# Statistics over two neighbouring tiles an instruction, the last two tiles loaded by channel halves, and a reordered start of the first layer

## The reference, cut to what matters

```python
def _gn(v, G=32, eps=1e-5):                       # mean and variance of an image over H, W and 12 channels
    g = v.reshape(B_, H_, W_, G, C_ // G)
    m = jnp.mean(g, axis=(1, 2, 4), keepdims=True)
    s = jnp.var(g, axis=(1, 2, 4), keepdims=True)
    return ((g - m) / jnp.sqrt(s + eps)).reshape(v.shape)

def conv_ref(x):                                  # WINDOW = (1, 5, 20), zero padded
    s = box_sum(x, 2, 5)                          # along the width
    num = box_sum(s * s, 3, 20)                   # along the channels
    d = box_sum(box_sum(x * x, 2, 5), 3, 20)
    denum = d * norm[None, :, :, None]            # norm: how many pixels of the width a window covers
    return jnp.nan_to_num(num / denum, nan=1.0)

x = x + conv_ref(_gn(x))                          # layer 0
x = x + conv_ref(_gn(x))                          # layer 1
```

## Time and profile before

| | before |
|---|---|
| median of 3 runs | 6088.15 us (6087.32 to 6090.02) |
| span of the profiled execution | 6085.2 us |
| TensorE busy | 5723.6 us (94%) |
| ScalarE busy | 5014.0 us (82%) |
| VectorE busy | 4144.7 us (68%) |
| GpSimd busy | 3546.7 us (58%) |
| DMA | 1007.81 MB, mean 166 GB/s |
| start of the first width unit | 323.31 us |
| start of the first channel unit | 331.46 us |

### The profile page before, as it was taken

The page is one execution under the profiler, slowest core; times in us unless marked ns, Lnnn a source line. Parts: engine busy times, 40 slices in busy tenths (PEclk is TensorE's granted clock), DMA queues, the critical chain, the costliest instruction groups (busy, mean ns, idle before and its releaser), DMA issues.

```text
span 6085.2 us, 139173 instructions
## 1 busy us (share of the span) xinstructions
PE 5723.6 (94%) x49196; PEld 5710.7 (94%) x49196; DVE 4144.7 (68%) x9033; ACT 5014.0 (82%) x8201; POOL 3546.7 (58%) x1043
## 2 busy tenths in 40 slices
PE   0089999999999999999999999999999999999999
PEld 0089999999999999999999999999999999999999
DVE  9988889988877766767667555555555555555555
ACT  0078888888888888888888888888888888888888
POOL 0056665566556666666665666666666666666665
PEclk9999999999999999999999999999999999999999
DMA  9946655556633433434334344343434434343343
GB/s 367 367 157 212 223 207 191 207 203 215 220 125 125 151 138 134 156 124 153 137 135 147 132 147 143 129 160 124 159 130 141 149 124 165 124 153 137 135 154 124
DMA packets 660641, 1007.81 MB, mean 166 GB/s; under 512 B 5168, under 2 KB 660528, under 8 KB 660528
## 3 DMA queue, kind: packets, MB, share of 16 engines
q1 hardware_dynamic: 660528, 1006.65, 47.1%
HBM read 603.98 MB, written 402.65 MB: 165 GB/s over the span
## 4 chain that ended last, share of the span: by engine, by line
PE 89%; DVE 8%; issue 2%; ACT 1%; DMA 0%; SPq 0%; DVEq 0%; POOL 0%; POOLq 0%; ACTq 0%
PE width_ps L468 43%; PE den_ps L492 23%; PE num_ps L492 23%; DVE out_stats L555 3%; DVE lane_mv L562 2%; DVE y_out L649 1%; DVE newton L631 1%; DVE recip L637 0%; DMA y_out<-in_x_dram 0%; DVE beside_stats L555 0%; ACT recip L398 0%; ACT recip L401 0%; SPq L198 0%; DVEq L555 0%; PE num_ps L443 0%
## 5 line engine op out<-in xcount | busy, mean ns | idle before, releaser
L312 POOL TENSOR_TENSOR centred<-x_in,mean_row 128x1536 f32<-128x1536 f32 x512 | 1771.0, 3459 | 1415.0 <-PE width_ps L468 1097.5
L321 POOL TENSOR_TENSOR y_out<-x_in,y_out 128x1536 f32<-128x1536 f32 x512 | 1771.4, 3460 | 1117.1 <-DVE y_out L649 1117.1
L631 DVE SCALAR_TENSOR_TENSOR newton<-den_ps,recip 128x384 f32<-128x384 f32 x2048 | 1110.7, 553 | 1884.7 <-ACT recip L401 1854.8
L492 PE MATMUL den_ps<-band_c,tT 128*128 128x138 f32 (+2 forms) x12288 | 1809.0, 283 | 9.6 <-DVE newton L631 9.6
L492 PE MATMUL num_ps<-band_c,sT 128*128 128x138 f32 (+2 forms) x12288 | 1732.6, 284 | 20.4 <-DVE recip L637 20.1
L468 PE MATMUL width_ps<-band_w,centred 128*128 128x130 f32 x12288 | 1628.3, 275 | 0.5 <-DVE rvar_col L620 0.5
L468 PE MATMUL width_ps<-band_wc,square 128*128 128x130 f32 x12288 | 1625.5, 275 | 0.0
L492 PEld LDWEIGHTS den_ps<-band_c,tT 128*128 128x128 f32 x12288 | 1608.9, 190 | 13.3 <-DVE newton L631 11.8
L492 PEld LDWEIGHTS num_ps<-band_c,sT 128*128 128x128 f32 x12288 | 1580.5, 190 | 27.7 <-DVE recip L637 22.9
L388 ACT ACTIVATE sT<-width_ps,rstd_col 128x512 f32<-128x512 f32 x1536 | 1035.8, 674 | 592.9 <-PE width_ps L468 592.9
L468 PEld LDWEIGHTS width_ps<-band_w,centred 128*128 128x128 f32 x12288 | 1507.0, 191 | 0.9 <-DVE rvar_col L620 0.9
(11 more groups left out here) (44 smaller groups left out, 302.8 us busy)
## 6 DMA issues: line engine op xcount, KB each, us to landing
x_in<-in_x_dram SPq DMA_DIRECT2D x80, 3072.0 KB, 11.0
first_layer_out<-y_out SPq DMA_DIRECT2D x64, 3072.0 KB, 18.2
x_in<-first_layer_out SPq DMA_DIRECT2D x64, 3072.0 KB, 10.9
out_dram<-y_out SPq DMA_DIRECT2D x63, 3072.0 KB, 18.1
beside<-in_x_dram SPq DMA_DIRECT2D x30, 3072.0 KB, 11.0
y_out<-in_x_dram SPq DMA_DIRECT2D x18, 3072.0 KB, 24.4
out_dram<-y_out SPq DMA_DIRECT2D x4, 768.0 KB, 3.5
```

What stands on the lines that cost most here:

```text
L312: nc.gpsimd.tensor_tensor(centred[e % 2][:], x_in[slot][:, g * PSEG:(g + 1) * PSEG, :], mean_row[ph % 2][:].unsqueeze(1).to_broadcast([P, ...
L321: nc.gpsimd.tensor_tensor(y_out[slot][:, g * PSEG:(g + 1) * PSEG, :], x_in[slot][:, g * PSEG:(g + 1) * PSEG, :], y_out[slot][:, g * PSEG:( ...
L492: last = nc.tensor.matmul(bank[:, lo:hi], data[:, k, at:at + P], band_c[k][:], start=(k == 0), stop=(k == KB - 1), skip_group_check=True)
L631: nc.vector.scalar_tensor_tensor(newton[:, i, :], den_ps[i % 3][:, 0:C], TINY, recip[par][:, i, :], ALU.add, ALU.mult).then_inc(den_used, 1)
```

## The change

It has these parts.

1. `x_in` and `y_out` become halves of `x_both` and `y_both` (same bytes, same places). In the opening one `bn_stats` reads both tiles of a buffer pair, 32 segments by 12 channels = 384 elements, in place of 192. VectorE waits for both tiles, and `tile_measured` now counts tile pairs; both buffers of a pair are given back together, when the pair is measured.
2. `opening_totals` takes the place of `lane_totals` in the opening: `bn_aggr` reads 48 numbers a group in place of 96.
3. The last two tiles (tile pair 15) are loaded by two transfers that each bring half of the channels (16 groups) of both tiles, in pieces of 768 bytes where the others move 1536 at a time. VectorE measures and folds the first 16 groups, then the other 16.
4. The loads of image 1's first tiles (`y_out[0]`, `beside`, `y_out[1]`) wait for `means_asked` 1, that is for the end of the opening's totals; before, each `y_out` waited for its buffer to be measured.
5. GpSimd centres row pair 1 only after `params_ready`. ScalarE does the squares of row pair 1 after the takes of row pair 0's first two channel blocks.
6. TensorE runs the first width unit of row pair 0 ahead of round 3 of the hand-over and the others right behind it; its wait for `params_ready` comes after all six. ScalarE's takes still wait for `params_ready`.

```diff
--- before.py
+++ after.py
@@ -59,6 +59,7 @@
     assert W == 2 * P and C == 3 * P and TILES % 4 == 0 and B == 2 and TILES >= 8
 
     SPLIT = TILES // 2
+    CUT = GROUPS // 2
     MID = SPLIT // 2
 
 
@@ -86,9 +87,12 @@
         def sem(name):
             return ctx.enter_context(nc.semaphore(name))
 
-        x_in = [sb(f"x_in{i}", [P, SEGS, C]) for i in range(2)]
-        y_out = [sb(f"y_out{i}", [P, SEGS, C]) for i in range(2)]
+        x_both = sb("x_both", [P, 2 * SEGS, C])
+        y_both = sb("y_both", [P, 2 * SEGS, C])
+        x_in = [x_both[:, i * SEGS:(i + 1) * SEGS, :] for i in range(2)]
+        y_out = [y_both[:, i * SEGS:(i + 1) * SEGS, :] for i in range(2)]
         stat_tiles = [x_in[0], x_in[1], y_out[0], y_out[1]]
+        stat_pairs = [x_both, y_both]
         centred = [sb(f"centred{i}", [P, PSEG, C]) for i in range(2)]
         square = [sb(f"square{i}", [P, PSEG, C]) for i in range(2)]
         sT = [sb(f"sT{i}", [P, KB, 2 * W]) for i in range(2)]
@@ -192,16 +196,23 @@
 
                 def measure_loads(i, lo):
                     for s in range(4):
-                        if lo > 0:
-
-                            sp.wait_ge(tile_measured, i * 4 + s - 3)
+                        if lo > 0 and s % 2 == 0:
+
+                            sp.wait_ge(tile_measured, i * 2 + s // 2 - 1)
+                        if lo == TILES // 4 - 1 and s >= 2:
+                            continue
                         sp.dma_start(stat_tiles[s][:], view[:, bass.ds((i * 4 + s) * SEGS, SEGS), :]
                                      ).then_inc(in_landed[s], 16)
-                looped(sp, TILES // 4, measure_loads, [0])
+                looped(sp, TILES // 4, measure_loads, [0, TILES // 4 - 1])
+
+                for part in range(2):
+                    cs = slice(part * CUT * CG, (part + 1) * CUT * CG)
+                    sp.dma_start(y_both[:, :, cs], view[:, (TILES - 2) * SEGS:TILES * SEGS, cs]
+                                 ).then_inc(in_landed[2 + part], 16)
 
                 for s in range(2):
 
-                    sp.wait_ge(tile_measured, TILES - 3 + s)
+                    sp.wait_ge(tile_measured, TILES // 2 - 1)
                     sp.dma_start(x_in[s][:], tiles_of(x, 0)[:, s * SEGS:(s + 1) * SEGS, :]
                                  ).then_inc(in_landed[s], 16)
                 def load_beside(n):
@@ -212,7 +223,7 @@
 
                 for s in range(UPFRONT):
 
-                    sp.wait_ge(tile_measured, TILES - 1 + s)
+                    sp.wait_ge(means_asked, 1)
                     sp.dma_start(y_out[s][:], tiles_of(x, 1)[:, s * SEGS:(s + 1) * SEGS, :]
                                  ).then_inc(in_landed[2 + s], 16)
                     if s == 0:
@@ -324,6 +335,8 @@
                                             ALU.subtract).then_inc(rows_out, 1)
 
                 centre(0, 0, 0, 0)
+
+                pool.wait_ge(params_ready, 1)
                 centre(0, 1, 0, 1)
                 for ph in range(NP_):
                     def tiles(i, lo):
@@ -415,12 +428,13 @@
                             take(ph1, p1, 1 - par, n, int(what[0] == "T"))
 
                 finish_logs(0)
-                for p in range(2):
-                    for half in range(2):
-                        squares(0, p, p, half)
+                for half in range(2):
+                    squares(0, 0, 0, half)
                 for k in range(KB):
                     take(0, 0, 0, k, 0)
                     take(0, 0, 0, k, 1)
+                    if k < 2:
+                        squares(0, 1, 1, k)
                 for ph in range(NP_):
                     def pairs(i, lo):
                         step(ph, i * 2, 0)
@@ -512,13 +526,15 @@
                         elif ph1 < NP_:
                             width_unit(ph1, p1, 1 - par, n, int(what[0] == "T"))
 
-                for part in (1, 2, 3):
+                for part in (1, 2):
                     finish_part(0, part)
-
-                pe.wait_ge(params_ready, 1)
                 for k in range(KB):
                     width_unit(0, 0, 0, k, 0)
+                    if k == 0:
+                        finish_part(0, 3)
                     width_unit(0, 0, 0, k, 1)
+
+                pe.wait_ge(params_ready, 1)
                 for ph in range(NP_):
                     def pairs(i, lo):
                         step(ph, i * 2, 0)
@@ -562,14 +578,35 @@
                         last = nc.vector.bn_aggr(lane_mv[b][:, half, g, :], stats[:, g, :])
                     link(last)
 
+                def opening_totals(half, groups):
+
+                    for g in groups:
+                        last = nc.vector.bn_aggr(lane_mv[0][:, half, g, :], out_stats[:, g, 0:SPLIT // 2 * 6])
+                    link(last)
+
+
+                def measure_two(base, i, s):
+
+                    for o in range(2):
+                        dve.wait_ge(in_landed[2 * s + o], (base + i + 1) * 16)
+                    measure(stat_pairs[s], range(GROUPS), out_stats, i * 2 + s).then_inc(tile_measured, 1)
 
                 for half in range(2):
-                    with dve.Fori(0, SPLIT // 4) as i:
-                        for s in range(4):
-                            dve.wait_ge(in_landed[s], (half * (SPLIT // 4) + i + 1) * 16)
-                            measure(stat_tiles[s], range(GROUPS), out_stats, i * 4 + s).then_inc(tile_measured, 1)
-                    dve.wait_ge(tile_measured, (half + 1) * SPLIT)
-                    lane_totals(0, half, range(GROUPS), out_stats)
+                    with dve.Fori(0, SPLIT // 4 - half) as i:
+                        for s in range(2):
+                            measure_two(half * (SPLIT // 4), i, s)
+                    if half == 0:
+                        dve.wait_ge(tile_measured, SPLIT // 2)
+                        opening_totals(0, range(GROUPS))
+
+                measure_two(SPLIT // 4, SPLIT // 4 - 1, 0)
+                for part in range(2):
+                    groups = range(part * CUT, (part + 1) * CUT)
+                    dve.wait_ge(in_landed[2 + part], TILES // 4 * 16)
+                    link(measure(y_both, groups, out_stats, SPLIT // 2 - 1))
+                    if part == 0:
+                        dve.wait_ge(tile_measured, TILES // 2 - 1)
+                    opening_totals(1, groups)
 
 
                 dve.wait_ge(bands_cut, 2 * HALVES + KB + 1)
@@ -721,7 +758,7 @@
 
                 dve.wait_ge(in_landed[2], (TILES // 4 + 1) * 16)
                 measure(y_out[0], range(GROUPS), beside_stats, 0).then_inc(tile_measured, 1)
-                dve.wait_ge(tile_measured, TILES + 1)
+                dve.wait_ge(tile_measured, TILES // 2)
                 for ph in range(NP_):
                     def tiles(i, lo):
                         for e in range(BODY):
```

## The result

The changed kernel takes 6078.42 us (median of 21 runs, 6077.46 to 6080.48) against 6087.15 us (21 runs, 6086.51 to 6090.15): ratio 0.9985, 95% interval 0.9978 to 0.9991. The gain is 8.7 us; 3.9 were forecast. The forecast time was 6084.2 us, 5.8 above what was measured: 4.8 of these are gain that was not forecast, and 1.0 is the kernel before, whose median of 3 runs (6088.15) stood 1.0 above that of the 21 runs here. The profiled execution has a span of 6078.8 us.

The account below looks back on a forecast made before the run. The opening, in which TensorE idles, was taken as bound by a buffer pair's round trip. Opening 1.1 us sooner plus hand-over 2.8 gave -3.9 us, 6084.2 us; own range 6078 to 6091, 8 in 10 within 6072 to 6101.

Parts of the forecast that it names:

- One instant decides: Whole kernel: the change is worth the shift of the first channel unit, from 331.46 to 327.5 us, -3.9 us.
- D0: First channel unit, at 331.46 us in the kernel before, behind which every engine goes on as before; forecast at 327.5.
- Prices: Opening on VectorE: 461 ns for statistics over 384 elements, 14.8 us a tile pair; 255 ns for totals over 48 numbers.
- The rival of a price by the instruction: Opening's totals: 64 totals stay at 450 ns each, +12.5 us, 6096.7 us; chance 0.20.
- the one of statistics that don't shorten: Opening's statistics: a cost for each of 16 segments, not for the instruction; +16.7 us, 6100.9 us; chance 0.06.
- The round trip binds: Opening: a buffer pair is measured, reissued and landed in 34.8 us for two tile pairs, 17.4 us a tile pair.
- L: Opening's loads: time from issue to landing of a buffer pair's two tiles, taken as 19.9 us, between 19.4 and 20.4.
- The last part: Opening's last tile pair: both halves there when VectorE needs them; opening ends at 309.9 us, not 311.0, gain 1.1 us.
- Hand-over: From the opening's end to the first channel unit: 20.4 us becomes 17.6, a gain of 2.8 us.
- Part 4: Later loads of image 1: VectorE waits 1.5 us for `y_out[0]`; cost nothing, but later arrivals show one to one.
- a sign of being wrong: After the opening: `newton` waiting for `y_out[0]` would show the forecast wrong; the first `newton` was due at 329.9 us.
- The rival in which the DMA never runs dry: Opening's loads: issue overlaps the running pair, so 16 pairs pass at 16.87 us; -22 us, 6066 us; chance 0.11.

Follow-up runs that it names:

- experiments 1 and 2: Changed kernel with a third buffer pair: 6070.95 us; changed kernel with two 192-element statistics for each of 384, buffers still given back by pairs: 6096.16 us.
- experiment 5: Parts 5 and 6 undone in the changed kernel: 6081.88 us; added to the kernel before, both 6085.01, part 5 alone 6085.13, part 6 alone 6086.94.
- experiments 6 and 8: Changed kernel, second centring started at the reciprocal roots: 6077.35 us; kernel with three buffer pairs, spread first-half totals and earlier image 1 loads: 6070.38 us.

## Why the prediction was right, and where it was short

- *One instant decides.* Right: the shift of D0 (9.1) is the shift of the medians (8.7) to within their 1 us, and in every experiment too. The time lies at the lower edge of the forecast's own range (6078 to 6091), and the gain is more than twice the forecast: the mechanism was right and its sizes were not, and all three misses below err the same way.
- *Prices.* Statistics of 384 elements: forecast 461 ns and 14.8 us a pair; measured 14.81. Totals: 255 ns forecast, 232 measured; 64 of them are 1.5 us. The rival of a price by the instruction is out, and so is the one of statistics that don't shorten.
- *The round trip binds.* Right in kind, shown by experiments 1 and 2. L was forecast at 19.9; on the path it was 19.4 to 19.7, mostly 19.55, nearly the lower bound, one tile's trip plus one more transfer. A round was 34.5 for 34.8: six trips, some 2 us. The row I had leaned to, 20.4 for the first two tiles, holds for that kernel alone: the four traces of kernels that measure tile by tile have the second tile at 21.1 to 21.3, the ten that measure by pairs at 20.3 to 20.6, with the same two tiles behind it in the queue (19.6 after its issue in the changed kernel). Pair 1 landed at 38.0, not 39.1, which I had taken over as if nothing had moved; with three buffer pairs it landed at 37.24, though more loads are queued behind it there (asked for at 20.77) and none in the changed kernel. So the queue behind a load explains neither difference, and the cause stays open. The fit of the Trainium skill, "DMA: Bandwidth & Descriptors", section on the anatomy of one DMA, that the prediction set beside the row, is of transfers issued from GpSimd, which the prediction does not say; these are SP's.
- *The last part.* From pair 14's landing to the end 37.4 for 38.4, the totals again. 768-byte pieces were 1.14 times as dear (326 for 373 GB/s), within 1 to 2, and hidden. By the Trainium skill, "DMA: Bandwidth & Descriptors", section on small descriptors, the prediction had estimated 1.06; the measurement decides. Together the opening ended at 305.3 for 309.9: 4.6 of the 4.8 us by which the gain was under-forecast (3.9 for 8.7). The steps that failed in size are these three: the trip, the first landing, the totals.
- *Hand-over.* 17.6 forecast, 17.1 measured; the stall that goes, the delay in round 3 (0.7 forecast, 0.5 by experiment 5) and the squares in between were right, and that the early width units are worth near nothing is shown by leaving either part out.
- *Part 4.* VectorE waited 1.96 us (1.5 forecast) and `newton` was 0.5 late, which the prediction had named as a sign of being wrong. That it would show one to one was wrong: experiments 6 and 8 move it, and every `divide` goes by D0.
- *The rival in which the DMA never runs dry* was no outcome of this change, but it is what the third buffer pair makes of it.

## What to carry to other kernels

When buffers are given back in larger units, work out the round trip (measure, ask, first byte, transfer, landing) before pricing the faster instruction; an engine that waits a little before every unit may still be on the loop. Two units in flight hold no lead, so every stall of the consumer is paid in full; a third one, from memory that is idle in that stage, was worth as much again as the whole change (-17.1 for -8.7). Look for small VectorE instructions that end exactly when a GpSimd operation does: holding back one such operation gave all of the hand-over's gain here. And read a change of one instant at several later operations: their shift told 0.1 us where medians told 1.

## What the runs showed of the hardware

- `bn_aggr` of 96 numbers starts every 0.45 us, of 48 every 0.232: (0.45 - 0.232)/48 = 4.5 ns a number and 13 ns beside.
- Loads in pieces of 768 bytes ran at 326 GB/s, of 1536 at 373, with the same 3072 KB a transfer.
- With the rate at 373 GB/s throughout, every third or fourth landing of a tile pair came 0.7 to 1 us late (pairs 17.6 to 17.8 us apart where the others are 16.87, in the kernels with three buffer pairs). The cause is open.
- A VectorE `tensor_tensor` of 128x32 took 3.36 us beside GpSimd's centring and 0.19 without it.
- At a granted clock of 0.50 a unit of width sums took 1.94 us, at 1.00 it took 1.06; but the first units behind the hand-over's idleness took 1.9 to 2.1 us too, where the stretch's clock reads 1.00 (the kernel before, 323.31 and 325.21).
